# A gated cross-layer and attention block on one core: context loaded first, block sums shared with ScalarE and GpSimd, first maxima taken from the unstacked operands, and a two-instruction layer norm on ScalarE

## What is computed

```python
xq = quant_dequant_act_1x128(layernorm(x))        # fp8 per row and block of 128
wq = quant_dequant_weight_128x128(ctx)            # fp8 per block of 128 x 128
x = x + tanh(g_xattn) * einsum('emk,enk->emn', xq, wq)
h = layernorm(x)
Q, K, V = heads of h @ (Wa * column scales)       # 16 heads of 32
y = causal_softmax(Q K^T / sqrt(32)) V
x = x + tanh(g_ffn) * (y @ Wp)
```

## Time and profile before

| | us |
|---|---|
| median of 3 runs (500.25 to 502.68) | 502.21 |
| the profiled execution's own time | 499.74 |
| its span, first to last instruction | 497.9 |
| PE busy / DVE busy in the span | 440.6 / 340.3 |
| ACT busy / POOL busy in the span | 255.7 / 151.1 |

### The profile page before, as it was taken

One profiled execution on the slowest core, in us unless ns is written; L12 is line 12 of the kernel. 1 busy time (PEld: TensorE's weight loads), 2 busy tenths in 40 slices (PEclk: granted clock), 3 DMA queues, 4 the chain that ended last, 5 costly groups with the idle time before them and its releaser, 6 DMA issues.

```text
span 497.9 us, 7913 instructions
## 1 busy us (share of the span) xinstructions
PE 440.6 (88%) x2536; PEld 317.1 (64%) x2536; DVE 340.3 (68%) x1122; ACT 255.7 (51%) x498; POOL 151.1 (30%) x278
## 2 busy tenths in 40 slices
PE   0375989998979999998969999999879999999996
...
DMA packets 27929, 42.62 MB, mean 86 GB/s; under 512 B 8272, under 2 KB 8528, under 8 KB 27888
## 3 DMA queue, kind: packets, MB, share of 16 engines
...
q0 software_dynamic: 192, 0.39, 0.3%
...
...
## 4 chain that ended last, share of the span: by engine, by line
PE 66%; DVE 24%; ACT 3%; issue 3%; DMA 2%; POOL 1%; SPq 0%; ACTq 0%; DVEq 0%; POOLq 0%
PE pv_bank L748 13%; DVE x_all L1201 10%; PE mm_bank L594 9%; PE mm_bank L595 8%; PE mm_bank L596 8%; PE exp_bank L734 6%; PE max_bank L717 5%; DVE max_bank L1230 5%; PE mm_bank L775 2%; PE mm_bank L777 2%; PE mm_bank L776 2%; PE turn_bank L610 2%; DVE bn L1208 2%; PE pv_bank L757 1%; DMA x_all<-in_x 1%
## 5 line engine op out<-in xcount | busy, mean ns | idle before, releaser
L1230 DVE CUSTOM_DVE_ANT_0 max_bank<-max_bank,causal 128x512 f32<-128x512 f32 (+3 forms) x256 | 121.0, 512 | 52.5 <-PE max_bank L717 52.0
L1002 ACT ACTIVATE work<-exp_bank 128x512 f32<-128x512 f32 (+1 forms) x192 | 94.9, 526 | 56.2 <-PE exp_bank L734 55.2
L512 POOL TENSOR_SCALAR_AFFINE_SELECT work<-work 128x384 f32<-128x384 f32 x64 | 33.4, 522 | 281.6 <-ACT work L1002 281.6
L748 PE MATMUL pv_bank<-work,v_aug 128*33 128x256 f32 (+3 forms) x512 | 78.9, 451 | 0.6 <-DVE work L1241 0.2
L734 PE MATMUL exp_bank<-q_stack,k_stack 97*128 97x512 f32 (+3 forms) x256 | 71.2, 341 | 7.6 <-ACT work L1002 6.5
L717 PE MATMUL max_bank<-k_stack,q_stack 96*128 96x512 f32 (+3 forms) x256 | 71.1, 338 | 2.4 <-DVE row_max L1230 1.8
L1201 DVE SCALAR_TENSOR_TENSOR x_all<-mm_bank,coef,x_all 128x128 f32<-128x128 f32 x224 | 61.5, 342 | 0.3
L748 PEld LDWEIGHTS pv_bank<-work,v_aug 128*33 128x33 f32 x512 | 29.7, 113 | 50.1 <-issue 42.1
L734 PEld LDWEIGHTS exp_bank<-q_stack,k_stack 97*128 97x128 f32 x256 | 45.6, 188 | 23.4 <-ACT work L1002 14.7
L594 PE MATMUL mm_bank<-xt_hi,w_hi 128*128 128x512 f32 x128 | 53.4, 417 | 0.7 <-ACT v_aug L981 0.7
L717 PEld LDWEIGHTS max_bank<-k_stack,q_stack 96*128 96x128 f32 x256 | 45.2, 191 | 12.7 <-DVE row_max L1230 3.7
...
## 6 DMA issues: line engine op xcount, KB each, us to landing
q_stack<-qk_hi SPq DMA_DIRECT2D x128, 64.0 KB, 2.0
...
```

Source lines behind the costliest of these rows:

```text
L512: pool.affine_select(out=three, in_=three, compare_op=ALU.is_ge, fill=0.0, base=0, pattern=[[0, 3], [1, P]], channel_multiplier=-1)
L748: last = pe.matmul(pv_bank[64 * j:64 * j + D + 1, P * m:T], v_aug[:, m, 2 * u + j, :], prob[j][:, PROB_COL[m]:PROB_COL[m] + T - P * m], st ...
L1002: act.activation(prob[j][:, UNIT_COL[k]:UNIT_COL[k] + UNIT_LEN[k]], exp_bank[(3 * j + k) % 2][:, 0:UNIT_LEN[k]], ACT.Exp, scale=SCALE).the ...
L1230: last = dve.tensor_tensor_reduce(max_bank[unit % 2][:, col:col + width], max_bank[unit % 2][:, col:col + width], causal[:, T - width:T], ...
```

## The change

1. SP loads the context before x; of the small loads, three are issued by ACT behind `part_sign` and eight by SP. In DVE's list the context maxima come first, and the statistics of x behind them.
2. The last quarter of the weights' Q and K columns is loaded later, into the space of the first; `first_x` lies in `v_aug`.
3. Of the first batch's sixteen block products, the last one of each tile is no longer added by DVE: ACT multiplies it by its coefficients (`s0` to `s3`, four instructions of 128 x 128) into `tile_buf`, and POOL adds the tile (`a0` to `a3`).
4. The four context turns of the start are copied by DVE (`f0` to `f3` there) instead of ACT, and the scales of x are made for two tiles at once (`G0`, `G1`).
5. The first maxima read `qk_hi` and `qk_lo` in place, 32 rows deep, with three products each, in six pieces `M0` to `M5` among the products of `k1`, so that they do not wait for stacked rows.
6. In the batches `L0` to `L3` move from DVE to ACT, two instructions each (subtract the mean, then scale).
7. All lists are written anew.

```diff
+            def layernorm_x(n, i):
+                if i == 0:
+                    act.wait_ge(s_rstd1, n + 1)
+                act.wait_ge(s_turn, 12 * n + i + 1)
+                buf = tile_buf[:, i, :]
+                act.activation(buf, x_tile(n, i), ACT.Identity, bias=shift1[:, i:i + 1]).then_inc(s_xc, 1)
+                act.wait_ge(s_xc, NT * (n - 1) + i + 1)
+                act.activation(buf, buf, ACT.Copy, scale=rstd1[:, i:i + 1]).then_inc(s_xn, 1)
+            def first_product(i):
+                act.wait_ge(s_coef, 1)
+                act.wait_ge(s_turn, i + 1)
+                act.wait_ge(s_cross, NK * i + NK)
+                for t in range(NT):
+                    last = act.activation(tile_buf[:, i, P * t:P * t + P], sum_bank(True, i, NK - 1)[:, P * t:P * t + P],
+                                          ACT.Copy, scale=coef[:, i, t, NK - 1:NK])
+                last.then_inc(s_fmul, 1)
+                elif kind == "a":
+                    pool.wait_ge(s_fmul, i + 1)
+                    pool.wait_ge(s_summed, 3 * i + 3)
+                    pool.tensor_tensor(x_tile(0, i), x_tile(0, i), tile_buf[:, i, :], ALU.add).then_inc(s_fadd, 1)
...
+                for i, col in MAX_UNITS[k]:
+                    width = P * (i + 1)
+                    dst, cols = max_bank[unit % 2][:, col:col + width], slice(P * i, P * i + P)
+                    pe.matmul(dst, qk_hi[rows, 0, 0, cols], qk_hi[rows, 0, 1, 0:width], start=True, stop=False)
+                    pe.matmul(dst, qk_lo[rows, 0, 0, cols], qk_hi[rows, 0, 1, 0:width], start=False, stop=False)
+                    last = pe.matmul(dst, qk_hi[rows, 0, 0, cols], qk_lo[rows, 0, 1, 0:width], start=False, stop=True)
+                last.then_inc(s_sm, 1)
...
-PE_FIRST = ("f0 f1 f2 f3 f4 S0 S1 S2 S3 f5 S4 S5 S6 f6 S7 S8 f7 S9 f8 S10 S11 S12 S13 S14 "
-     "S15 f9 f10 v0 f11 v1 q0 B0 B1 k0 V2 q1 M0 k1 M1 M2")
+PE_FIRST = ("f0 f1 f2 f3 f4 S0 S1 S2 S3 f5 S4 S5 f6 S6 S7 S8 S9 S10 S11 f7 f8 S12 S13 S14 "
+     "f9 S15 f10 v0.012 f11 v0.3 v1.0 q0.0 v1.1 q0.1 B0 q0.23 v1.2 B1 v1.3 k0.01 V2.0 k0.2 V2.12 k0.3 V2.3 q1.0 M0 q1.1 "
+     "M1 q1.23 M2 k1.01 M3 M4 k1.2 M5 k1.3")
-ACT_FIRST = ("a0 C0 C1 C2 f0 d0 f1 C3 f2 C4 b0 f3 f4 C5 C6 f5 a1 C7 f6 b1 f7 N0 f8 a2 "
-     "a3 N1 f9 N2 b2 f10 N3 b3 v0 f11 v1 q0 k0 c0 V2 D0 c1 p0 q1 D1 k1 c2 c3")
+ACT_FIRST = ("d0 C0 a0 C1 a1 b0 a2 C2 C3 b1 C4 C5 f4 C6 f5 s0 f6 s1 C7 a3 f7 s2 e3 N0 "
+     "N1 b2 f8 s3 f9 N2 N3 f10 b3 v0 f11 q0 c0 k0 v1 V2 D0 D1 c1 q1 c2 k1 c3 p0")
-DVE_FIRST = ("x0 w0 x1 x2 x3 t0 t1 L0 L1 t2 t3 L2 A0 A1 T0 F0 F1 L3 F2 F3 T1 T2 c0 S0 "
-     "S1 S2 S3 b0 S4 S5 S6 S7 S8 b1 S9 S10 S11 S12 b2 S13 h0 S14 S15 b3 T3 h1 u0 u1 "
-     "h2 u2 h3 u3 B0 q0 B1 k0 M0 q1 M1 M2 k1")
+DVE_FIRST = ("t0 t1 t2 t3 A0 x0 A1 x1 x2 x3 w0 L0 F0 T0 L1 F1 L2 F2 L3 G0 T1 T2 F3 f0 "
+     "f1 f2 G1 f3 c0 S0 S1 S2 S4 S5 S6 S8 b0 S9 S10 b1 u0 u1 S12 S13 b2 S14 u2 h0 "
+     "b3 h1 T3 h2 h3 u3 B0 B1 q0 k0 M0 M1 M2 M3 M4 M5 q1 k1")
-POOL_FIRST = ("i0 s0 s1 s2 s3 s4 s5 o0 s6 j0 s7 r0 j1 l0 l1 r1 l2 l3 r2 r3 j2 j3 g0 g1 "
-     "D0 g2 D1 g3 p0")
+POOL_FIRST = ("s0 i0 s1 l0 s2 s3 s4 o0 s5 j0 l1 s6 s7 l2 a0 j1 a1 v0 r0 l3 a2 r1 r2 a3 "
+     "r3 j2 j3 g0 g1 D0 g2 g3 D1 p0")
...
 DVE_STEPS = [
-    "max0 max1 max2 max3 x0 x1 max4 max5 x2",
-    "x3 max0 max1 L0 Q2 max2 max3 m0 max4 L1 norm max5 L2",
-    "m1 L3 max0 e0 K2 max1 max2 m2 m3 e1 norm max3 max4 Q3 max5",
-    "K3 max0 max1 S0 S1 max2 max3 S2 S3 S4 norm max4 max5",
-    "b0 S5 max0 S6 S7 max1 b1 max2 S8 max3 max4 S9 norm max5",
-    "S10 max0 max1 S11 t0 S12 max2 max3 H0 S13 max4 S14 b2 S15 t1 t2 max5 t3 norm b3 H1",
-    "A0 max0 max1 max2 max3 max4 max5 H2 norm",
-    "H3 A1 norm q0 k0 q1",
+    "max0 max1 max2 max3 max4 max5 x0 x1 x2 x3",
+    "max0 max1 Q2 max2 m0 m1 max3 max4 K2 max5 norm",
+    "max0 max1 e0 max2 m2 max3 m3 e1 max4 Q3 max5 norm",
+    "max0 max1 max2 K3 S0 max3 S1 S2 max4 max5 S3 S4 S5 norm",
+    "max0 S6 max1 max2 S7 b0 b1 S8 max3 S9 max4 norm max5 S10 S11",
+    "max0 t0 max1 b2 t1 S12 t2 max2 max3 S13 max4 t3 max5 norm S14 A0",
+    "S15 b3 H0 max0 max1 max2 H1 max3 max4 H2 max5 norm A1",
+    "H3 q0 norm",
 ]
...
 END_LAST = {
-    "PE": "Z1 Z2 pv Z3 back Z4 Z5 z3 Z6 Z7 Z8 Z9 Z10 Z11",
+    "PE": "pv Z3 back Z4 Z5 z3 Z6 Z7 Z8 Z9 Z10 Z11",
```

More of the change, by code:

```diff
@@ L136 @@
+PE_END = ("pv k1.0 V0.0 back k1.1 V0.1 y0 k1.23 V0.2 max0 y1 V0.3 V1.01 max1 max2 V1.23 V2.0 max3 V2.12 max4 V2.3 y2 max5 y3 "
+     "O0 O1 O2 O3")
+ACT_END = "c0 copy k1 y0 V0 y1 c1 V1 c2 V2 y2 c3 y3"
+DVE_END = "k0 q1 norm k1 max0 max1 y0 max2 y1 max3 max4 max5 y2 y3 O0 O1 O2 O3"
 END_LAST = {
-    "PE": "Z1 Z2 pv Z3 back Z4 Z5 z3 Z6 Z7 Z8 Z9 Z10 Z11",
+    "PE": "pv Z3 back Z4 Z5 z3 Z6 Z7 Z8 Z9 Z10 Z11",
     "ACT": "copy z3",
-    "DVE": "z2 Z1 Z2 norm Z3 z3 Z8 Z9 Z10 Z11",
+    "DVE": "z2 Z2 norm Z3 z3 Z8 Z9 Z10 Z11",
@@ L520, in weight_lo @@
             def weight_lo(k):
-                raw, tail = raw_w[k], tails[k]
-                v0 = 2 * H * DS
                 pool.wait_ge(s_wtailhi, k + 1)
@@ L711, in scores_for_max @@
                         pe.wait_ge(s_pstack[s], 48)
-                if unit >= 2 or not first:
-                    pe.wait_ge(s_max, 48 * n + 6 * u + unit - 1)
+                pe.wait_ge(s_max, 48 * n + 6 * u + unit - 1)
                 bank = max_bank[unit % 2]
```

218 lines of the change are left out of this document (125 added, 93 removed), and 77 rows, old and new, of tables (ACT_LAST, ACT_STEPS, DVE_LAST, PE_LAST).

## The result

Slower. The changed kernel takes 508.22 us (median), the kernel before 501.56 in the runs beside it: ratio 1.0131, 95% interval 1.0108 to 1.0154. The forecast was 501.2 and "the same"; 508.2 lies just outside its range. Medians are over all runs, while ratios and intervals leave out those in a second, slower state of the chip: one of the changed kernel's five (515.18; the other four have a median of 507.6), and one or two of six in seven of the experiments, c1's profiled run among them. The profiled execution has its own time of 508.22 and a span of 506.4, against 499.74 and 497.9.

The account below looks back on a forecast made before the run. PE bounds most of the kernel, DVE the block-sum stretches. Start +2.0 net and three batches -3.3 give -1.3 on the 502.2 median, stated as 501.2 ("the same"); range 496.3 to 507.8.

Parts of the forecast that it names:

- From q0 to the first rowmax ... 20.9 against 20.5: End of the start: unstacked maxima spend in products what they win in waits; 20.9 us against 20.5, +0.4.
- Three batches: -3.3: Step 5 to 6 of three batches: 1.1 us back per batch from the slow stretch, bounds 0 and -5.
- the 0.7 that I had taken off for W0: Another turn, W0, ahead of the first rowmax: 0.7 us of work that the batch then need not do.
- The start up to q0: Start of the kernel: q0 at 61.8 us, 2.3 later than before.
- POOL's 11.8: Start, context first: POOL begins scaling at 11.8 us, 4.3 earlier than before.
- L0's 15.9: Start, x statistics after the context's: inverse deviation done at 15.9 us instead of 11.6, so L0 4.3 later.
- The first sum: Start: first sum at 32.6 us against 31.68 before, with DVE's stops taken at half the old size.
- the rival's value, 34.1: Start: with the port lock stopping nearly every L, T, G and c0 on DVE, first sum at 34.1 us.
- From the first sum to `q0`: Start: b3 22.3 us after the first sum, then 6.9 for r3, j2 and j3 on POOL before q0.
- The rival "slower": Port stops from L0 to c0 cost the start 4.0, batches win 1: 505.2; with exp0 delayed 1.5 a batch, 508. Chance 0.28.
- signs of being wrong: First sum before 31 or after 34; no DVE stops of 1 us; exp0 late with PE idle; batch clock below 0.9.
- the third rival: Batches: the hole only moves to step 4 or 5, the start's +2.0 remains: 504.2. Shares the 0.37 for "same".

Follow-up runs that it names:

- c1: The changed kernel with f0 to f3 copied by ACT, four places around S15 exchanged and p0 ahead of q1 in the start: 509.37 us, ratio 1.0167.
- e2: The changed kernel with the first maxima's products taken over 128 rows instead of 32: 505.60 us, ratio 1.0094.
- g4: The changed kernel with the first maxima over 128 rows, v_aug's clearing behind r3 and p0 ahead of q1: 505.68 us, ratio 1.0101.
- e5: The changed kernel with three weight pieces of POOL moved behind the scaling of the last x tiles in the start: 509.58 us, ratio 1.0184.
- e7: The changed kernel with copies f0 to f3 of the turned context tiles on ACT instead of DVE: 508.35 us, ratio 1.0137.
- g2: The changed kernel with v_aug's clearing behind r3, S15, s3, a3 and b3 in exchanged places, and f11 ahead of v0: 513.05 us, ratio 1.0240.
- r1: The changed kernel with part 5 alone undone, first maxima read from stacked operands, one product each: 508.10 us, ratio 1.0152.
- e1: The changed kernel with p0 moved ahead of q1 on ACT in the start instead of last: 506.94 us, ratio 1.0106.
- h1: The kernel before (old start, stacked first maxima) with the new lists of the batches and last batch and layer norm on ACT: 498.85 us, ratio 0.9968.
- h2: The old start with the new order of the batches, but L0 to L3 back on DVE as one instruction each: 502.40 us, ratio 1.0034.
- l1: The kernel before with part 6 alone, L0 to L3 of the batches as two ACT instructions each: 502.05 us, ratio 1.0035.
- g1: The changed kernel with v_aug's clearing moved behind r3 instead of ahead of r0 on POOL: 508.95 us, ratio 1.0138.

## Why the prediction was wrong

**What failed.** Two steps. The first is "From q0 to the first rowmax ... 20.9 against 20.5": it is 26.0. Of the 5.1 missing, 1.8 are the changes of row depth, which I priced at nothing, and 1.4 the low clock, which the sum did not have either; e2 and g4 against e5, e7 and g2 show both sizes, though not why the clock fell. The last 1.9 (22.8 less 20.9) is ordinary, and the steps of e2's timeline add up to it: the wait for V2's copy is 0.5 longer than my 0.7, the projections' matmuls take 16.5 and not 15.7, the products of the first maxima 3.7 and not 3.4, and the small turns and the first maxima of the next step 0.7, for which I had 0.4. I had written that the unstacked maxima spend in products what they win in waits. r1 says that the balance was right and both sides too small: stacked, the wait was 1.73 and not 0.61.

The second is "Three batches: -3.3": they took 2.4 longer. The profile's span is 9.8 us over my sum (8.5 longer where I had 1.3 shorter): 4.9 of these lie ahead of the first `rowmax` (87.6 against 82.7), 5.7 in the three batches, and the last batch gave 0.8 more than the 0.7 that I had taken off for W0.

**What I had not listed.** p0 as ACT's last piece: 1.2 us in step 0, shown by e1. I had read ACT's new list for what stands behind waits, but not for what stands ahead of `neg`.

**The start up to q0** came out right in its sum by luck: 61.56 against 61.8, since two errors cancel. POOL's 11.8 and L0's 15.9 held (11.68, 15.64). The first sum was 2.1 late: I had halved the stops on DVE, and the rival's value, 34.1, was nearer to 34.66. T0's copy and predicated copy took 1.11 and 1.03, the coefficients 2.34. By the Trainium skill, "SBUF — State Buffer", "Who interferes with whom", I expected nearly all of these instructions to stop. The trace agrees in part: of the three copies of 128x256 one took 1.11, one 0.69 and one 0.29, and two of the four L took their usual 0.55. In e5 moved POOL work moved the stops and did not remove them. From the first sum to `q0` the kernel then took 26.9 where I had 29.2. The four ACT instructions of s took 1.14 where I took 1.0; an estimate from the Trainium skill, "ScalarE: Activation LUTs", "What ACT_TABLE_LOAD costs", gave 1.2.

**The rival "slower"** named a time near the measured one (508) by another mechanism: of its 4.0 us at the port 3.0 came true and 0.9 of them were won back, and `exp0` was never late by L0 and L1. Its own terms, 505.2 and 1.5 for each of three batches, add up to 509.7. My own sum has a slip too: 502.2 less 1.3 is 500.9, not 501.2. Two of the signs of being wrong came: a first sum after 34, and a clock below 0.9 in a batch.

**The batches.** -3.3 was wrong in every kernel with the new lists. The fourteen profiles of the table that have them need 320.8 to 324.8 us for the three batches without the first batch's step 0, 322.4 in the mean, and the kernel before 323.1; its step 0 is 1.0 longer in all of them, even without p0. So the new order gave about nothing there. What it gave lies in the last batch, for which I had 0: 83.8 to 84.3 us against 85.9, and this is h1's gain as well. The hole only moved, as the third rival had it. PE's timeline of the changed kernel, second batch, and its windows around step 5:

```profile
261.65 0.57 PE L664 MATMUL mm_bank<-wt_hi,wt_lo 128*128 128x512 f32 x1 [1.36 <-DVE x_all L1260]
```

```profile
259.40:263.40 4.00, 2.64 (x15) 2.15 (x13) 3.97 (x14) 2.45 (x5) 0.77 (x2) 0.82 0.00 0
263.40:267.40 4.00, 3.29 (x13) 2.28 (x11) 3.97 (x17) 2.67 (x6) 0.76 (x2) 0.76 0.00 0
```

The wait of 3.09 before `rowmax` of step 6 is gone, but a block product of step 5 waits 1.36 for DVE's sum, DVE is full (3.97 of 4.00 us), and the clock falls there instead (0.82 and 0.76). Pricing the layer norm on ACT at nothing was wrong too: in the new order it is worth 0.7% or 3.3 us (h2 against h1, by their ratios), of which h2's timeline places 1.5 in step 1, and in the old order it costs (l1).

**What stays open.** No kernel with the new start came within 4 us of the kernel before. In g4, with the depth and p0 undone, the second `rowmax` is still 7.0 us behind that of h1. `q0` is 3.8 of it (1.1 by a later L0 than in the changed kernel), and 2.05 are three quarters of v1, which the old start had done before `q0`. Which part delays `q0` is not settled: undone or repaired one by one, parts 1 and 4 and the chain behind S15 gave way to the next wait. That several chains end within a microsecond or two of each other is what e7, g1 and g2 show. Nor is it settled why the clock fell in seven of ten profiles with 32-row maxima and not in the three others.
